# Deformable sampling on one core: small VectorE steps taken once per tile of 128 points, the four large ones in halves

## The reference

```python
q, k, v   = dwconv3x3(x @ w_qkv + b_qkv)                 # 128 channels each
mask      = sigmoid(conv1x1(pconv(q)))                    # 9 taps
for i in range(4):                                        # groups, dilation 2i+1
    off    = conv1x1(pconv_i(q))                          # 9 taps, y and x
    k_i    = bilinear(k[group i], base + off) * mask      # 4 corners a tap, 32 channels
    v_i    = bilinear(v[group i], base + off) * mask
attn = softmax(einsum('bgnc,bgckn->bgnk', q * 32**-0.5, k_s), axis=-1)   # over the 9 taps
out  = einsum('bgnk,bgckn->bgnc', attn, v_s) @ w_proj + b_proj
x    = x + out
```

## Time and profile before

| | us |
|---|---|
| median of 3 runs | 9669.9 (9655.2 to 9689.3) |
| span of the profiled execution | 9686.6 |
| first gather starts, last gather starts | 216.8, 6828.6 |
| busy DVE, POOL, PE, ACT | 6067.7 (63%), 4575.1 (47%), 3083.5 (32%), 1385.9 (14%) |

### The profile page before, as it was taken

How to read it: one execution, slowest core, us unless ns; L and a number is a source line. 1 busy time by engine, 2 the same in 40 slices (tenths; PEclk the granted TensorE clock), 3 DMA queues, 4 the chain that set the end, 5 groups by cost and what they waited for, 6 DMA issues and landing times. The chain is left out here.

```text
span 9686.6 us, 108210 instructions
## 1 busy us (share of the span) xinstructions
PE 3083.5 (32%) x41476; PEld 2213.2 (23%) x41476; DVE 6067.7 (63%) x8431; ACT 1385.9 (14%) x2582; POOL 4575.1 (47%) x4747
## 2 busy tenths in 40 slices
PE   4102101021001101021001100101255476999997
PEld 2001000010001000010001000100233365788885
DVE  6567675776775557685875557545673565555554
ACT  1000000000000000000000000000122232444442
POOL 0766666666677567666777667766100000000000
PEclk7555555565555555555555555555677788999998
DMA  4434345343353234343453234323123443222224
GB/s 86 121 93 111 95 111 145 95 111 92 109 155 99 80 94 126 90 114 91 111 155 99 86 97 121 102 88 96 38 45 127 110 105 90 60 66 67 66 66 179
DMA packets 822930, 966.58 MB, mean 100 GB/s; under 512 B 283028, under 2 KB 643560, under 8 KB 817896
## 3 DMA queue, kind: packets, MB, share of 16 engines
q0 software_dynamic: 221184, 604.27, 21.1%
q1 hardware_dynamic: 573880, 321.25, 13.4%
q10 hardware_dynamic: 27440, 34.87, 1.0%
HBM read 797.64 MB, written 155.99 MB: 98 GB/s over the span
## 5 line engine op out<-in xcount | busy, mean ns | idle before, releaser
L511 POOL DMA_INDIRECT l_rec<-records,l_row x4608 | 4518.7, 981 | 2309.6 <-issue 1421.4
L1070 DVE TENSOR_REDUCE l_att_t<-l_rec 128x64 f32<-128x2304 f32 x256 | 1025.5, 4006 | 8.8
L2323 DVE COPY l3p_mix<-l3p_ps 128x512 f32<-128x512 f32 x1024 | 659.9, 686 | 576.1 <-PE l3p_ps L2199 576.1
L668 PE MATMUL l_pso<-l_wo,l_att_c 128*128 128x128 f32 x256 | 101.9, 501 | 2560.9 <-issue 1684.5
L1051 DVE TENSOR_TENSOR l_rec<-l_rec,l_psv 128x2304 f32<-128x2304 f32 x256 | 653.7, 2553 | 202.5 <-DMA l_rec<-records,l_row 88.7
L678 PE MATMUL l_pso<-l_id,l_att_t 128*128 128x128 f32 x128 | 58.0, 453 | 2114.1 <-DVE l_att_t L1070 1472.7
L1068 DVE TENSOR_TENSOR l_rec<-l_rec,l_psv 128x2304 f32<-128x2304 f32 x256 | 653.7, 2554 | 100.6 <-DVE l_psv L1066 67.8
L780 ACT ACTIVATE l_prob<-l_score 128x18 f32<-128x18 f32 x256 | 56.1, 219 | 4381.0 <-DVE l_score L1056 1442.2
L1052 DVE TENSOR_REDUCE l_psv<-l_rec 128x72 f32<-128x2304 f32 x256 | 655.6, 2561 | 11.4 <-remote 1.7
L668 PEld LDWEIGHTS l_pso<-l_wo,l_att_c 128*128 128x128 f32 x256 | 64.2, 312 | 2607.0 <-issue 1717.9
L2285 ACT ACTIVATE l3p_mix<-l3p_ps 128x512 f32<-128x512 f32 x1024 | 557.7, 597 | 662.8 <-PE l3p_ps L2199 662.8
(11 more groups left out here) (359 smaller groups left out, 6394.6 us busy)
## 6 DMA issues: line engine op xcount, KB each, us to landing
l_rec<-records,l_row POOLq DMA_INDIRECT x4608
l2b_w<-l_w SPq DMA_DIRECT2D x32, 1024.0 KB, 10.9
records<-l_area SPq DMA_DIRECT2D x48, 512.0 KB
l_row<-meta SPq DMA_DIRECT2D x124, 154.0 KB
l_x_hat<-l3a_xout ACTq DMA_DIRECT2D x32, 512.0 KB, 4.6
l3p_xin<-l_x_hat SPq DMA_DIRECT2D x128, 128.0 KB, 3.1
l_y_raw<-l3p_yr SPq DMA_DIRECT2D x64, 256.0 KB, 3.4
l3p_yin<-l_y_raw SPq DMA_DIRECT2D x128, 128.0 KB, 2.9
```

Source lines behind the costliest of these rows:

```text
L511: pool.indirect_dma_start(out=rec[:, r, k, :], out_offset=None, in_=records[b].rearrange("r c d -> r (c d)"), in_offset=bass.IndirectOffse ...
L668: pe.matmul(ps_p, att_c[:, :], wo0_s[:, :], start=True, stop=True).then_inc(s_proj, 1)
L1070: step(dve.tensor_reduce(att_t[two][:, HG * HC * h:HG * HC * (h + 1)].rearrange("p (g d) -> p g d", g=HG), values.rearrange("p g m d -> p ...
L2323: dve.tensor_copy(mix[t.side(0)][:, x:x + 2, :, :].rearrange("p x c e -> p (x c e)"), ps[(2 * q + h) % 3][:, 1, :]).then_inc(s_setd, 1)
```

## The change

- DVE takes the small steps once for all 36 taps: corner weights (144 columns), sum over corners, a minimum over 9 taps, and later reciprocal, normalisation and corner weights. The four large steps are still done in halves: keys 0, sum 0, keys 1, sum 1, small steps, values 0, sum 0, values 1, sum 1.
- The queries are stored with negative sign, so that scores are negated; the group's minimum `low` is the bias of the exponential. ACT computes, for each of the 4 groups, `exp(-score + low)` with `accum_out` for the sum. The subtraction (L1056) and the sum of exponentials (L1062) leave DVE.
- ACT copies the next tile's queries into PSUM, behind the exponentials (`ask`); the copy leaves DVE (L1049).
- DVE has 16 steps a tile in place of 27, and a few of them no longer make the next instruction wait (`low`, the second add, the sums of values).
- Both halves of a tile are now in use until its sums: `summed(t, 0)` comes two steps before `summed(t, 1)`.
- PE and ACT take a tile's two slots after that tile's transpose, `turned` and projection, and ACT's exponentials of the next tile follow both slots.

```diff
-                        ACT.Copy, scale=float(HC) ** -0.5)
+                        ACT.Copy, scale=-float(HC) ** -0.5)
...
@@ tensor
             for t in range(TILES):
-                if t:
-                    project(t - 1)
-                next(side)
-                next(side)
-                pe.wait_ge(s_dve, summed(t, 1))
+                pe.wait_ge(s_dve, summed(t))
                 pe.transpose(ps_a, att_t[t % 2][:, :], id_s[:, :]).then_inc(s_att, 1)
-            project(TILES - 1)
+                project(t)
+                next(side)
+                next(side)
@@ scalar
+            def ask(t):
+                act.wait_ge(s_row[t % AHEAD], 16 * (t // AHEAD + 1))
+                return act.activation(ps_q, row[t % AHEAD][:, QUERY:META], ACT.Copy)
+
+            def weigh(t):
+                act.wait_ge(s_dve, scored(t))
+                for g in range(GROUPS):
+                    k = slice(TAPS * g, TAPS * g + TAPS)
+                    ins = act.activation(prob[:, k], score[:, k], ACT.Exp, bias=low[:, g:g + 1], scale=-1.0, accum_out=total[:, g:g + 1])
+                if t + 1 < TILES:
+                    ins = ask(t + 1)
+                ins.then_inc(s_exp, 1)
...
             for t in range(TILES):
-                for h in range(2):
-                    act.wait_ge(s_dve, scored(t, h))
-                    act.activation(prob[:, :], score[:, :], ACT.Exp).then_inc(s_exp, 1)
-                    if h == 0 and t >= 1:
-                        turned(t - 1)
-                    if h == 0 and t >= 2:
-                        store(t - 2)
-                    next(side)
+                weigh(t)
+                if t >= 1:
+                    store(t - 1)
+                turned(t)
+                next(side)
+                next(side)
@@ vector, tile t
                 for h in range(2):
+                    dve.wait_ge(s_rec[2 * two + h], 16 * HT * (t // 2 + 1))
                     step(dve.tensor_tensor(keys, keys, asked.broadcast_to([P, HG, TAPS * CORNERS, HC]), ALU.mult))
+                    step(dve.tensor_reduce(flat[:, HT * CORNERS * h:HT * CORNERS * (h + 1)], rec[:, 2 * two + h, :, :].rearrange(
+                        "p k (c d) -> p (k c) d", c=CORNERS)[:, :, 0:HC], AX, ALU.add))
+                step(dve.tensor_tensor(flat, flat, wgt, ALU.mult))
+                step(dve.tensor_reduce(score[:, :], dots[:, :, :], AX, ALU.add))
+                dve.tensor_reduce(low[:, :], score[:, :].rearrange("p (g k) -> p g k", k=TAPS), AX, ALU.min).then_inc(s_dve, 1)
+                if t >= 1:
+                    add(t - 1, step)
+                dve.wait_ge(s_exp, t + 1)
+                step(dve.reciprocal(inverse, total[:, :]))
+                step(dve.tensor_tensor(share, prob[:, :], inverse broadcast over taps, ALU.mult))
+                step(dve.tensor_tensor(ps_w, wgt, share broadcast over corners, ALU.mult))
+                for h in range(2):
+                    step(dve.tensor_tensor(values, values, part broadcast over channels, ALU.mult))
+                    dve.tensor_reduce(att_t[two][half h], values, AX, ALU.add).then_inc(s_dve, 1)
+                next(side)
+                next(side)
```

More of the change, by code:

```diff
@@ L177, in first_layers @@
         att_t = [st.sb(f"att_t{i}", [P, C]) for i in range(2)]
[L178 to L179 removed]
+        score = st.sb("score", [P, GT])
+        prob = st.sb("prob", [P, GT])
+        low = st.sb("low", [P, GROUPS])
+        total = st.sb("total", [P, GROUPS])
         att_c = st.sb("att_c", [P, P])
@@ L715, in points @@
                                 for t in range(AHEAD):
-                                    act.activation(row[t][:, QUERY:META], bank[:, t * P:t * P + P], ACT.Copy, scale=float(HC) ** -0.5)
+                                    act.activation(row[t][:, QUERY:META], bank[:, t * P:t * P + P], ACT.Copy, scale=-float(HC) ** -0.5)
                             if at == 0 and b in (1, 2):
@@ L1030, in add @@
                 step(dve.tensor_tensor(done[t % 2][:, :], ps_p, res[t % 2][:, :], ALU.add))
-                step(dve.tensor_tensor(done[t % 2][:, :], done[t % 2][:, :], bo0_s[:, :], ALU.add))
+                dve.tensor_tensor(done[t % 2][:, :], done[t % 2][:, :], bo0_s[:, :], ALU.add).then_inc(s_dve, 1)
+                step.n += 1
             whole(points(0))
@@ L1036, in _ @@
                 s, two = t % AHEAD, t % 2
+                step = Chain(dve, s_dve, s_gate[2], begun(t))
+                view = [rec[:, 2 * two + h, :, :].rearrange("p (g k) (c d) -> p g (k c) d", k=TAPS, c=CORNERS) for h in range(2)]
+                HG = GROUPS // 2
+                wgt = row[s][:, GT:QUERY]
+                flat = dots[:, :, :].rearrange("p k c -> p (k c)")
+                if t == 0:
+                    dve.wait_ge(s_asked, 1)
                 for h in range(2):
-                    r = 2 * two + h
@@ L1039, in _ @@
-                    step = Chain(dve, s_dve, s_gate[2], begun(t, h))
-                    view = rec[:, r, :, :].rearrange("p (g k) (c d) -> p g (k c) d", k=TAPS, c=CORNERS)
+                    keys = view[h][:, :, :, 0:HC]
                     asked = ps_q[:, HG * HC * h:HG * HC * (h + 1)].rearrange("p (g o d) -> p g o d", o=1, d=HC)
-                    keys, values = view[:, :, :, 0:HC], view[:, :, :, HC:2 * HC]
-                    wgt = row[s][:, GT + HT * CORNERS * h:GT + HT * CORNERS * (h + 1)]
@@ L1058, in _ @@
-                    if h == 1 and t >= 1:
-                        add(t - 1, step)
-                        assert step.base + step.n == added(t - 1)
-                    dve.wait_ge(s_exp, 2 * t + h + 1)
-                    step(dve.tensor_reduce(total[:, :], pg, AX, ALU.add))
-                    step(dve.reciprocal(total[:, :], total[:, :]))
-                    step(dve.tensor_tensor(share.rearrange("p (g k) -> p g k", k=TAPS), pg,
-                                           total[:, :].unsqueeze(2).broadcast_to([P, HG, TAPS]), ALU.mult))
@@ new lines, in _ @@
+                step(dve.tensor_tensor(ps_w.rearrange("p (k c) -> p k c", c=CORNERS), wgt.rearrange("p (k c) -> p k c", c=CORNERS),
+                                       share.unsqueeze(2).broadcast_to([P, GT, CORNERS]), ALU.mult))
+                for h in range(2):
+                    values = view[h][:, :, :, HC:2 * HC]
+                    part = ps_w[:, HT * CORNERS * h:HT * CORNERS * (h + 1)].rearrange("p (g m) -> p g m", g=HG)
+                    step(dve.tensor_tensor(values, values, part.unsqueeze(3).broadcast_to([P, HG, TAPS * CORNERS, HC]), ALU.mult))
+                    dve.tensor_reduce(att_t[two][:, HG * HC * h:HG * HC * (h + 1)].rearrange("p (g d) -> p g d", g=HG),
+                                      values.rearrange("p g m d -> p g d m"), AX, ALU.add).then_inc(s_dve, 1)
+                    step.n += 1
```

63 lines of the change are left out of this document (24 added, 39 removed).

## The result

The changed kernel takes 9792.8 us (median of 4 runs, 9785.8 to 9800.2), the kernel before 9679.6 in the runs beside it (9655.2 to 9691.7): a ratio of 1.0115, 95% interval 1.0099 to 1.013. The forecast was 9563, faster. It is 1.15% slower, inside the range and on its other side.

The account below looks back on a forecast made before the run. The loop was taken as bound by POOL at 46.1 us a tile and by DVE where it falls behind, paced by instruction count. 9686.6 - 230 + 123 = 9580, less 17 to the median, gave 9563 us; range 9370 to 9800.

Parts of the forecast that it names:

- 4608 x 1.281 = 5901 us, 46.1 us a tile, which the change does not touch: POOL's gathers in the loop: mean 0.981 us plus a fixed 0.30 us each, taken as the pace.
- 711 us of waits: POOL's waits in the loop, 671 us of them for DVE; the gain could not exceed 711 us.
- The check on ten tiles: Tiles from 2993.1 to 3613.3 us: 159 us behind less the allowance of 53 is 106, against 112 found.
- The filter tiles: DVE tiles with two filter slots, paced by instruction count: 63.0 us would become 44, below POOL's 46.1.
- Rival 3: DVE's pace is not one of instruction count: filter tiles gain 1.1 us, 9870 or about 9750 us; chance 0.10.
- Three: -230 us: Three rounds of `points`: 60 us of POOL waits each in place of 137, together 230 us saved.
- The exponentials, 1.3 us of waiting: ACT's four activations and copy take 1.9 us against 0.21; DVE waits some 1.3 us a tile.
- The handover between `qkv` tiles, 30 us: From ACT's exponentials to the next `qkv` job: 2 + 14 + 14 = 30 us, 16 more than now.
- The late slots, +30 a round for `qkv`, three places of 20 us a round in `linear`: Slots after the projection: 30 us a `qkv` round; `linear` +60, net +41 a round, +123 us for three.
- Rival 2: Late slots cost more than small steps give: 9740 to 9920 us, likeliest 9760, half price giving half; chance 0.25.
- DVE end of the loop: nothing: DVE's work at the end of the loop was to add no time.
- POOL's waits near 600: Sign that the forecast is right: POOL's waits near 600 us, fewest after filters, more around `qkv` slots and in `linear`.

Follow-up runs that it names:

- experiment 5: The kernel of experiment 1 with all side slots run after the loop and rows and records of image 0 for all tiles; loop of 6423 us.
- experiment 1: The changed kernel, but PE takes a tile's slots before waiting for its sum and ACT before copying the transpose; 9659.6 us, 0.9974.
- experiment 2: The kernel before, 27 steps kept, with PE and ACT slots as in the changed kernel and DVE's slots after the tile; 9868.2 us, 1.0191.
- experiment 4: The changed kernel with the reciprocal repeated, 11 more small steps, 27 steps a tile; 9878.7 us, 1.0203.
- run 27: Not a run label: part of the words "run 27 us ahead", the some 27 us that POOL may be ahead of its lasting pace.
- experiment 13: The kernel of experiment 5 with a semaphore increment on POOL behind each gather; loop of 6453 us.

## Why the prediction was wrong, step by step

The kernels that do the whole work, by the place of the slots and by the steps (ratio to the kernel before):

| slots on PE and ACT | 27 steps | 16 steps |
|---|---|---|
| early | 1.0015 (0.9995 to 1.0034) | 0.9974 (0.996 to 0.9988) |
| as before | 1 | 1.0007 (0.9992 to 1.0022) |
| late | 1.0191 (1.0163 to 1.0219) | 1.0115 (1.0099 to 1.013) |

By these ratios the new steps are worth some 40 us with early slots, nothing with the slots as before, and 74 us with late ones; the late slots cost some 105 us against the order of before and 136 against the early one with the new steps, 185 and 170 with the old ones. So the two parts of the change do not simply add up.

- **"4608 x 1.281 = 5901 us, 46.1 us a tile, which the change does not touch", with 711 us of waits above it: this step failed, and the gain with it.** The floor of the loop is 6423 us (experiment 5). Before the change the loop was 190 us above it, not 711. While DVE holds POOL up, POOL wins back what it was ahead, so up to 5.4 us of waiting a tile cost nothing; more than the some 27 us that it was ahead can't be won back. With fewer waits the same gathers get slower: waits less 36 us and busy plus 91 after the change, less 200 and plus 120 in experiment 1. With more waits they get quicker: in experiments 2 and 4 POOL waits 891 and 954 us for DVE and its gathers are busy for 4479 and 4463 us. The trace of before had the sign. The mean gather of 981 ns lies above the 0.95 us of the neighbours that were taken for the pace, and in four tiles before 646 us, up to where POOL has not once waited for DVE, a window of POOL in that trace has 203.3 us, or 50.8 a tile, with 151 of them busy:

```profile
442.60:645.90 203.30, 151.15 (x145) 0.51 0.34 99
```

- **The check on ten tiles, 106 us against 112, agreed by luck.** The 112 us belong to the whole round of 1000 us; in the ten tiles POOL waits 91 us for DVE, and with 50.4 us a tile the same working gives 620.2 - 504 - 53 = 63.
- **The filter tiles, "44, below POOL's 46.1": right in length,** 40.9 to 45.2 us where two of the prediction's tiles 5 to 8 stood (the four take 56.3, 40.9, 45.2 and 50.4, together 193 in place of 238). Rival 3 is refuted by experiment 4. But below 50.4 a shorter tile is worth something only where DVE has fallen far behind. "Three: -230 us" for the `points` rounds rests on quick tiles winning back time from the 711 us. What the new steps gave in the whole program was nothing in the order of before (0.9992 to 1.0022) and 74 us with late slots.
- **The exponentials, 1.3 us of waiting: right in kind,** 0.94 us in the timeline above. The four activations start 0.29 us apart, as each accumulator read runs beside the next of them:

```profile
1678.53 0.29 ACT L775 ACTIVATE l_prob<-l_score,l_low 128x9 f32<-128x9 f32 x1
1678.72 0.19 ACT L775 ACTIVATION_READ_ACCUMULATOR l_prob<-l_score,l_low 128x1 f32 x1
1678.81 0.29 ACT L775 ACTIVATE l_prob<-l_score,l_low 128x9 f32<-128x9 f32 x1
```

- **The handover between `qkv` tiles, 30 us: too high.** From the exponential at 1678.53 to the next job it is 18.8 us, against 14.1: the copy of the transpose comes 15.9 us after it, near the 2 + 14 of the sum, but from there to the first job it is 2.9 us where 14 were set.

```profile
1694.41 0.28 ACT L782 ACTIVATE l_att_c<-l_pso 128x128 f32<-128x128 f32 x1 [14.49 <-PE l_pso L676]
1697.28 0.69 ACT L706 ACTIVATE l_area<-l_ps,l_bn 128x512 f32<-128x512 f32 x1 [2.59 <-issue]
```

- **The late slots, +30 a round for `qkv`, three places of 20 us a round in `linear`: mis-sized place by place, and not too low in the sum.** Over three rounds that is 90 and 180 us, besides the offset slots, and the time shows 105 to 136 us with the new steps. By place and over three rounds, DVE's waits grew at L983 by 62 us, which is the 3 x 20; at L991 by 150, which is far more; at the output (L1010) by 4, where 60 were set; at the offset slots (L866) by 50. The rest stands at the reciprocal. Which of these waits cost time and which POOL won back, by the first point, was not shown one by one. Rival 2, "the late start costs more than the small steps give", names what happened, and its "likeliest 9760" was closest to 9793. That closeness is luck in part: its sum too counted the steps' gain as 230 us, and the half price was a choice.
- **"DVE end of the loop: nothing": wrong by 20 us.**
- **"POOL's waits near 600": about right** (635), but not for the forecast's reason, as the time went the other way. It is the wrong quantity to watch: waits and gathers have to be added.

The sum by what the runs show: the late slots +185 us with the old steps, the new steps -74 in that order, together +111. The chance of 0.61 for faster rested on a floor of 1.281 us a gather, which is a mean over quick and slow gathers (0.981) plus a gap read from one quick pair (0.30).

Open: why a gather has a lasting pace of 1.40 us and how POOL comes to run 27 us ahead of it. DVE's paced steps also stand 1.40 us apart (experiment 4), but the increments of experiment 13 cost almost nothing, so a common cause is not shown. Open too is why early slots help with 16 steps and not with 27.

## What to carry to other kernels

Take an engine's floor from a long stretch in which nothing holds it up, not from two neighbouring instructions or from a mean that has pauses in it: if it issues more quickly for a while than it can for long, its waits are partly repayments, and removing them gives less than their sum. When work is moved behind another engine's result, price every slot in which someone waits for it, not only those that show a wait already. Change an order and the steps in separate runs: here the steps with early slots were 0.26% faster than before and the same steps with late slots 1.15% slower.

## What the hardware showed that was not expected

- POOL's indirect gathers have two paces: 0.946 us and 0.30 between them for some 180 in a row, then 1.40 us each on average. It stays 50.4 us for 36 gathers with 128 or 256 floats a record and with 64 or 128 records, and it is per gather. A pause of 24.1 us in four tiles costs 2.6 us.
- Where it binds, single gathers show as 1.10, 1.24 and 1.80 us long; with a semaphore increment behind each they stay at 0.94 and the gaps between them grow instead.
- DVE's small steps with a wait each come 1.40 us apart, some 0.70, in filter tiles with 27 of them, which take 63.0 us; with 16 such a tile takes 40.9, with 40.9 and 38.9 us busy. Whether the instructions or their waits set the pace is open.
